# Constants folded into a clamp, and the last gate product ahead of the last but one up product

## The reference, cut to what matters

```python
def act_quant(x):
    scale = 127.0 / jnp.clip(jnp.max(jnp.abs(x), axis=-1, keepdims=True), EPS)
    q = jnp.clip(jnp.round(x * scale), -128.0, 127.0) / scale
    return x + jax.lax.stop_gradient(q - x)

def h_bitlinear(x, w):
    xq = act_quant(fwht(x))
    wq = weight_quant(w)
    return jnp.einsum('bsh,oh->bso', xq, wq)

gate = h_bitlinear(hidden_states, w_gate)
up = h_bitlinear(hidden_states, w_up)
return h_bitlinear(jax.nn.silu(gate) * up, w_down)
```

## Time and profile before

| | us |
|---|---|
| median of 3 runs | 481.35 |
| the three runs | 481.11 to 481.57 |
| the profiled execution | 481.52 |
| its span, first to last instruction | 479.7 |

### The profile page before, as it was taken

How to read it: one execution, slowest core, us unless ns; L and a number is a source line. 1 busy time by engine, 2 the same in 40 slices (tenths; PEclk the granted TensorE clock), 3 DMA queues, 4 the chain that set the end, 5 groups by cost and what they waited for, 6 DMA issues and landing times.

```text
span 479.7 us, 9075 instructions
## 1 busy us (share of the span) xinstructions
PE 462.8 (96%) x3130; PEld 299.9 (63%) x3130; DVE 392.5 (82%) x765; ACT 292.8 (61%) x465; POOL 211.8 (44%) x314
## 2 busy tenths in 40 slices
PE   8999999999999999989999999999999999989997
PEld 7665656665666434468844479854468874469664
DVE  4889988798968749859997967998885999879892
ACT  3578886677768668877645517653616653648470
POOL 4245455978987544654005834201936200840000
PEclk9999999999999999999999999999999999999999
DMA  6999220021022023000100550100371110153086
GB/s 195 305 348 338 81 53 15 20 57 25 13 66 78 12 56 132 1 1 13 23 11 3 109 138 27 22 11 0 61 158 44 24 23 0 22 88 69 0 134 218
DMA packets 68183, 35.90 MB, mean 75 GB/s; under 512 B 50288, under 2 KB 62960, under 8 KB 68144
## 3 DMA queue, kind: packets, MB, share of 16 engines
q1 hardware_dynamic: 67728, 34.61, 28.2%
q10 hardware_dynamic: 416, 0.79, 0.5%
HBM read 19.26 MB, written 4.19 MB: 49 GB/s over the span
## 4 chain that ended last, share of the span: by engine, by line
PE 63%; DVE 20%; issue 7%; DMA 5%; ACT 3%; SPq 1%; DVEq 0%
PE ps L835 11%; PE ps L884 9%; PE ps L610 9%; PE ps L593 9%; PE ps L636 6%; PE ps L863 5%; DVE y_split L1371 4%; PE ps L653 4%; DVE mz L1410 3%; DVE wst L1391 3%; DMA reg_rest<-reg 2%; PE ps L618 2%; DVE f_max L1337 2%; DVE wst L1396 2%; PE ps L690 1%
## 5 line engine op out<-in xcount | busy, mean ns | idle before, releaser
L835 PE MATMUL ps<-wst 128*128 128x512 bf16 x512 | 112.5, 379 | 0.5 <-DMA wst<-q_b 0.5
L1224 DVE TENSOR_REDUCE reg<-ps 128x4 f32<-128x512 f32 x128 | 82.0, 685 | 25.1 <-PE ps L610 24.3
L555 POOL TENSOR_TENSOR reg_rest<-reg_rest,z_sc 128x1024 f32<-128x1024 f32 x24 | 48.2, 2045 | 92.0 <-DVE z_sc L1434 92.0
L959 ACT ACTIVATE reg<-ps 128x1024 f32<-128x1024 f32 x64 | 65.5, 1023 | 35.7 <-PE ps L618 35.3
L610 PE MATMUL ps<-reg 32*128 32x256 f32 x512 | 86.7, 400 | 0.5 <-DVE reg L1224 0.3
L835 PEld LDWEIGHTS ps<-wst 128*128 128x128 bf16 x512 | 49.5, 98 | 59.6 <-issue 1.8
L593 PE MATMUL ps<-reg 32*128 32x512 f32 x256 | 71.9, 639 | 0.0
L1091 ACT ACTIVATE wst<-wst 128x512 f32<-128x512 f32 x64 | 40.0, 626 | 51.9 <-DVE wst L1391 51.5
L863 PE MATMUL ps<-had_f,wst 128*128 128x128 f32 x512 | 67.1, 275 | 1.3 <-DVE wst L1396 1.3
L863 PEld LDWEIGHTS ps<-had_f,wst 128*128 128x128 f32 x512 | 64.1, 191 | 4.4 <-DVE wst L1396 1.8
L610 PEld LDWEIGHTS ps<-reg 32*128 32x128 f32 x512 | 58.6, 184 | 5.7 <-issue 1.1
(11 more groups left out here) (167 smaller groups left out, 747.4 us busy)
## 6 DMA issues: line engine op xcount, KB each, us to landing
wst<-in_w SPq DMA_DIRECT2D x16, 512.0 KB, 8.2
reg<-in_w SPq DMA_DIRECT2D x8, 512.0 KB, 5.4
out<-x_all SPq DMA_DIRECT2D x16, 256.0 KB, 2.1
x_all<-in_x SPq DMA_DIRECT2D x3, 1024.0 KB, 9.9
reg<-in_k_t SPq DMA_DIRECT2D x32, 32.0 KB, 2.3
reg<-in_v SPq DMA_DIRECT2D x4, 256.0 KB, 3.5
x_all<-in_x ACTq DMA_DIRECT2D x1, 512.0 KB, 4.3
reg_rest<-reg SPq DMA_TRANSPOSE x20, 3.2
```

The source lines that it names most:

```text
L835: last = pe.matmul(ps[:, banks[ob % n], :], tern_gu[:, ob // 2, m, j, P * (ob % 2):P * (ob % 2) + P], q1_t[:, j, :], start=(j == 0), stop= ...
L959: act.activation(probs[:, 2 * j:2 * j + 2, :], ps[:, bank:bank + 2, :], ACT.Exp, scale=D ** -0.5).then_inc(sem("exp_done"), 1)
L1224: dve.tensor_reduce(neg_max[n % 2][:, g:g + 2, i + m, :], ps[:, row_banks(r) + m, :].rearrange("p (g a t) -> p g a t", g=2, a=2), AX_X, AL ...
```

## The change

Three edits. In input_peak and early_peak the clamp now multiplies the maximum by 1/127 and clamps at EPS/(127/sqrt(512)) so that its reciprocal is the scale itself; the operation that multiplied the reciprocal (L1346, L1280) is gone, and the output scales take the constant 1/sqrt(512) back. f_c counts four per batch, POOL's early_scales included.

In chain the same is done, and the last two operations, a tensor_tensor of 64x8 (L1427) and a tensor_scalar that spreads its result to 64x128 (L1429), become one tensor_tensor of 64x128 whose two inputs are both spread. The tensor_scalar of the output scales gets a second constant.

In every gate_up the four matmuls of g15 stand ahead of those of u14: the end reads g14, g15, u14, u15. This is in each of the four units; DVE's and ACT's orders stay.

```diff
@@ early_scales
-                pool.wait_ge(sem("f_c"), 5 * tb + 5)
+                pool.wait_ge(sem("f_c"), 4 * tb + 4)
@@ new, called by gate_up
+            def rows(u, chain, ob, m, name, banks, used):
+
+                n = len(banks)
+                if ob >= n:
+                    pe.wait_ge(sem(used), u.times(NC, ob + 1 - n))
+                elif chain is not None and banks[ob] > 5:
+                    pe.wait_ge(sem("z_out"), chain.times(16, 16))
+                for j in range(NJ):
+                    last = pe.matmul(ps[:, banks[ob % n], :], tern_gu[:, ob // 2, m, j, P * (ob % 2):P * (ob % 2) + P],
+                                     q1_t[:, j, :], start=(j == 0), stop=(j == NJ - 1))
+                last.then_inc(sem(name), 1)
@@ gate_up
-                    for m, name, banks, used in ((0, "g_done", G_BANKS, "gs_done"), (1, "u_done", U_BANKS, "h_done")):
...
+                    if ob < NC - 1:
+                        rows(u, chain, ob, 0, "g_done", G_BANKS, "gs_done")
+                    if ob == NC - 2:
+                        rows(u, chain, NC - 1, 0, "g_done", G_BANKS, "gs_done")
+                    rows(u, chain, ob, 1, "u_done", U_BANKS, "h_done")
@@ input_peak (early_peak and early_round alike)
-                dve.wait_ge(sem("f_c"), n.times(5, 1))
-                dve.tensor_scalar(f_max[:, 1:2], f_max[:, 0:1], C_E, EPS, ALU.mult, ALU.max).then_inc(sem("f_c"), 1)
-                dve.wait_ge(sem("f_c"), n.times(5, 2))
+                dve.wait_ge(sem("f_c"), n.times(4, 1))
+                dve.tensor_scalar(f_max[:, 1:2], f_max[:, 0:1], 1.0 / QMAX, EPS / (QMAX * C_E), ALU.mult, ALU.max).then_inc(sem("f_c"), 1)
+                dve.wait_ge(sem("f_c"), n.times(4, 2))
                 dve.reciprocal(f_max[:, 2:3], f_max[:, 1:2]).then_inc(sem("f_c"), 1)
-                dve.tensor_scalar(f_max[:, 4:6], wsc[:, 0:2], f_max[:, 1:2], 1.0 / QMAX, ALU.mult, ALU.mult
+                dve.tensor_scalar(f_max[:, 4:6], wsc[:, 0:2], f_max[:, 1:2], C_E, ALU.mult, ALU.mult
                                   ).then_inc(sem("f_c"), 1)
-                dve.wait_ge(sem("f_c"), n.times(5, 4))
-                dve.tensor_scalar(f_max[:, 3:4], f_max[:, 2:3], QMAX * C_E, None, ALU.mult).then_inc(sem("f_c"), 1)
-                dve.wait_ge(sem("f_c"), n.times(5, 5))
-                dve.tensor_scalar(q_int, ps[:, bank, :], f_max[:, 3:4], MAGIC, ALU.mult, ALU.add
+                dve.wait_ge(sem("f_c"), n.times(4, 4))
+                dve.tensor_scalar(q_int, ps[:, bank, :], f_max[:, 2:3], MAGIC, ALU.mult, ALU.add
                                   ).then_inc(sem("f_qf"), 1)
@@ chain
-                dve.tensor_scalar(cz[:, 2, :], cz[:, 1, :], C_I, EPS, ALU.mult, ALU.max).then_inc(c, 1)
...
+                dve.tensor_scalar(cz[:, 2, :], cz[:, 1, :], 1.0 / QMAX, EPS / (QMAX * C_I), ALU.mult, ALU.max).then_inc(c, 1)
...
                 dve.reciprocal(cz[:, 3, :], cz[:, 2, :]).then_inc(c, 1)
-                dve.tensor_scalar(cz[:, 4, :], cz[:, 2, :], wsd_tg[0:NG, :], None, ALU.mult).then_inc(sem("c_qs"), 1)
-                dve.wait_ge(c, u.times(5, 4))
-                dve.tensor_tensor(cz[:, 5, :], cz[:, 3, :], su[:, 1, :], ALU.mult).then_inc(c, 1)
-                dve.wait_ge(c, u.times(5, 5))
-                dve.tensor_scalar(q_sc[:, :, :], cz[:, 5, :].unsqueeze(2).broadcast_to([NG, T8, NC]), QMAX * C_I, None,
-                                  ALU.mult).then_inc(sem("c_qs"), 1)
+                dve.tensor_scalar(cz[:, 4, :], cz[:, 2, :], wsd_tg[0:NG, :], QMAX * C_I, ALU.mult, ALU.mult
+                                  ).then_inc(sem("c_qs"), 1)
+                dve.wait_ge(c, u.times(4, 4))
+                dve.tensor_tensor(q_sc[:, :, :], cz[:, 3, :].unsqueeze(2).broadcast_to([NG, T8, NC]),
+                                  su[:, 1, :].unsqueeze(2).broadcast_to([NG, T8, NC]), ALU.mult).then_inc(sem("c_qs"), 1)
```

More of the change, by code:

```diff
@@ L827, in gate_up @@
                         pe.wait_ge(sem("signed"), ob + 2)
-                    for m, name, banks, used in ((0, "g_done", G_BANKS, "gs_done"), (1, "u_done", U_BANKS, "h_done")):
-                        n = len(banks)
-                        if ob >= n:
-                            pe.wait_ge(sem(used), u.times(NC, ob + 1 - n))
-                        elif chain is not None and banks[ob] > 5:
-                            pe.wait_ge(sem("z_out"), chain.times(16, 16))
-                        for j in range(NJ):
-                            last = pe.matmul(ps[:, banks[ob % n], :], tern_gu[:, ob // 2, m, j, P * (ob % 2):P * (ob % 2) + P],
-                                             q1_t[:, j, :], start=(j == 0), stop=(j == NJ - 1))
-                        last.then_inc(sem(name), 1)
+                    if ob < NC - 1:
[3 more added lines that the diff above has]
+                    rows(u, chain, ob, 1, "u_done", U_BANKS, "h_done")
                     if chain is not None and ob == 4:
```

20 lines of the change are left out of this document (9 added, 11 removed).

## The result

The changed kernel takes 478.51 us (median of 4 runs, 478.15 to 478.60). The kernel before took 481.46 us beside it (481.11 to 481.59). The ratio is 0.9938 with a 95% interval of 0.9923 to 0.9954: 2.95 us faster. The forecast was 1.06 us faster, with a range that ended at 479.3, so the sign was right and the size was not: the time lies 0.8 us outside the range, beside the rival in which all steps count (478.58). The profiled execution of the changed kernel has a span of 476.7 us, where that of before has 479.7, and the full clock.

The account below looks back on a forecast made before the run. PE was taken to bound the kernel, with DVE counting only where PE waits. 3 x (0.19 + 0.13) + 0.10 = 1.06 us takes the median from 481.35 to 480.29; range 479.3 to 481.1.

Parts of the forecast that it names:

- the rival in which all steps count: No other engine holds anything back, so every removed DVE step counts: gain 2.77 us, median 478.58; chance 0.05.
- What bounds the kernel: Whole kernel: PE is busy 96% of the span, so a DVE edit pays only where PE waits for DVE.
- the four early operations that go give 0: Attention, early_peak: PE is packed, so removing four operations gains 0; without that cover, 4 x 0.19 us.
- tb 0: gain 0: Each transform, input_peak: input_round ends with POOL's butterflies, so DVE only waits longer and the 0.19 us gains 0.
- tb 1: gain 0: Each transform: earlier L1357 waits for POOL's L540 or leaves L1358 and L1359 behind it; at best 0.05, taken as 0.
- tb 2 and tb 3: 0.19 together: Each transform: DVE gains 0.19 us at each, but low(15) waits for ACT, so only 0.19 reaches chain.
- The end of chain: 0.13: Last two operations of chain, 0.41 us, become one tensor_tensor of 0.28 us: gain 0.13 us in each of three units.
- more of DVE's time counts: Rival: tb 1 keeps its 0.19 and PE uses 0.16 us slack; 0.48 per transform, median 479.81; chance 0.20.
- g15 ahead of u14: 0.10: First unit's gate_up end: silu(15) starts right behind ACT's sign, gaining 0.06 to 0.15 us, taken as 0.10; elsewhere 0.
- The wait for the DMA ahead of the kept product unchanged: Behind gate_up in the loop and last unit: the transposing DMA hangs on silu(12), which nothing moves; gain 0.
- The rival on the transposing DMAs: DMA ahead of project lands like the slowest, losing 1.6 us in each loop turn: 483.49; chance of slower 0.05.
- The new wait of g15 on gate(13): PE in gate_up: the first 0.87 us of such a wait only eat the wait for the DMA; cost nothing.

## Why the prediction missed

Term by term, in the order of its working:

- **What bounds the kernel.** PE does, and DVE counts where PE waits for it: right. The statement that through the attention it is PE alone, packed, was wrong, and it is the first step that failed. It was read off PE's matmul rows, whose ends are modelled, and these hid a wait of PE for DVE's maximum at three of the four early chains. The step "the four early operations that go give 0" measured 0.57 us in the changed kernel (0.51 with that edit alone). Its own bound, "4 x 0.19 us if that cover were gone", would have been near.
- **tb 0: gain 0.** Right: put back, the operation costs 0.02 to 0.04 us.
- **tb 1: gain 0.** This is the second step that failed, the one in the transform. The text named both ways it could go and allowed "at best 0.05" for the second. The second happened: q_b went ahead of L540, diag waited in its place, but DVE's next low came 0.22 us earlier after the transform's start (17.70 to 17.48), all of the 0.19 that was removed. My error was to put diag and m8u at their full length behind the end of L540. Diag was held while L540 ran and ended only 0.08 us behind it (226.92 against 225.93 + 0.91 = 226.84), so the low starts 0.14 us behind L540's end; before, with q_b as the one that was held, it was 0.54 (227.73 against 227.19).
- **tb 2 and tb 3: 0.19 together.** Right in mechanism: tb 3 put back costs 0.02 us, and low(15) waits 0.18 us for ACT, which the forecast had at 0.2. With tb 1's part first_had of tb 3 came earlier by the slack that the rival had worked out: 0.39 us behind the product ahead of it became 0.23.
- **The end of chain: 0.13.** Right: the merged operation takes 0.28 us, and the edit alone gives 0.10 to 0.11 in a transform stretch.
- **So a transform stretch** gives 0.53 to 0.54, not 0.32. The rival "more of DVE's time counts" had 0.48 and was the true case for this part; I gave it a chance of 0.20 because I trusted the lock between DVE and POOL to hold the end fixed.
- **g15 ahead of u14: 0.10.** 0.17 measured, alone and in the whole. Silu(15) stood behind the sign, as said. Everything here comes 0.36 us earlier through the attention and the start, the sign too (207.43 to 207.07). Silu(15) went from 208.62 to 208.11, 0.15 more than that, and starts 0.10 us before the sign's end: that is the upper end of the 0.06 to 0.15 that I had allowed.
- **The wait for the DMA ahead of the kept product unchanged: 0.78 missed.** This is the third step that failed, and the largest of the terms that were put at nothing. I had treated the landing as a property of the place. It was one of two slow landings of the earlier trace rows that stood on the path, with 3.98 us where 3.2 is the median. The other, 4.81 us in the last unit (issued at 461.03), has a 16 KB packet in its flight too. It takes 4.72 us in the changed kernel, so it gave the change little: PE's weight loads wait 0.56 us for it before and 0.48 after. The rival on the transposing DMAs had the right suspect and the wrong sign: such a landing can get worse by a shift of instructions, and also better. The new wait of g15 on gate(13), costed at nothing, is real, 0.34 us in the first turn of the loop, and was one of the signs of being wrong; it cost nothing there, as it only ate the wait for the DMA. In the kept unit DVE's gates are now what PE waits for, 0.81 us ahead of the product, as in the kernels without the swap.
- **Sum.** Expected: 3 x (0.19 + 0.13) + 0.10 = 1.06. Measured: 0.53 + 0.54 + 0.58 + 0.17 = 1.82 for these terms, and 0.57 + 0.78 = 1.35 for the two that had none, less 0.21 at the start: 2.96. Had the range allowed for the DMA's landing at its median, 0.8 us, it would just have held the time.

## What to carry to other kernels

Where an engine looks packed, look at its weight loads or at the starts of its instructions before you cost another engine's edit at nothing: here waits that the matmul rows hid gave 0.57 us at three places. When an awaited DMA takes longer than its kind, look for a fetch of instructions in its flight, and at the lengths of its single packets; an edit that changes the number of instructions can move it in or out, by 0.2 to 1.3 us, so a difference of that size needs its place in the trace before it is put down to the edit. And where a wait on the path is removed, ask which chain it had hidden: here 0.64 of 0.85 us came back behind POOL until one operation group of 1.15 us was moved into idle time.

## What the runs showed of the hardware

DVE's instructions come in single packets of 8 KB, about one for 130 of them; single packets of 16 KB, once for 78 to 161 matmuls, are taken as PE's. With one of them in its flight the transposing DMA took 3.44 to 4.01 us, with both 4.47, and with none 3.2; with one, 18 to 22 packets took over 0.3 us, where none did without a fetch; issued 1.7 us earlier behind chain_back, it took 4.76 and 4.96 with PE's. Memsets of no use in the first 10 us made the kernel before shorter by 0.78 us at 423 us and the changed one longer by 1.26, of which 0.23 to 0.57 goes with PE's fetch. Where a DVE and a POOL operation on SBUF come together, a shift of DVE's start from just behind to 0.14 us ahead of POOL's moved the long duration from the first DVE operation to the second, and 0.2 us were gained by it.
